# Second feed-forward pass of a conv-attention block: the last inner tile as f16 parts made by GpSimd

## What is computed

```python
def _bitlinear(x, W, b):
    y = einsum('btc,oc->bto', x, sign(W - groupmean(W))) + b
    # in 5 groups of 6 images: gamma = max|y| of the group
    return clip(y * 128 / (gamma + 1e-5), -128 + 1e-5, 128 - 1e-5)

def _L1_ffn_ref(x, W1, b1, W2, b2):       # 96 -> 384 -> 96
    h = _bitlinear(x, W1, b1)
    h = gelu(h, approximate=False)
    return _bitlinear(h, W2, b2)          # images 30 and 31 get zeros
```

## Time and profile before

| what | us |
|---|---|
| median of 3 runs (865.66 to 874.0) | 866.55 |
| the profiled execution | 865.46 |
| its span, first to last instruction | 863.7 |
| PE busy | 801.2 (93%) |
| DVE busy | 642.9 (74%) |
| ACT busy | 448.0 (52%) |
| POOL busy | 190.0 (22%) |

### The profile page before, as it was taken

The page is one execution under the profiler, slowest core; times in us unless marked ns, Lnnn a source line. Parts: engine busy times, 40 slices in busy tenths (PEclk is TensorE's granted clock), DMA queues, the critical chain, the costliest instruction groups (busy, mean ns, idle before and its releaser), DMA issues.

```text
span 863.7 us, 17964 instructions
## 1 busy us (share of the span) xinstructions
PE 801.2 (93%) x6053; PEld 621.3 (72%) x6053; DVE 642.9 (74%) x1998; ACT 448.0 (52%) x619; POOL 190.0 (22%) x218
## 2 busy tenths in 40 slices
PE   1889799999999999999999999999999799999991
PEld 1456478888888888888888888888888655555550
DVE  3875377877777777777777777777677457988997
ACT  0232335445445445445445445445444299988981
POOL 2750022322222322322322322322322000000000
PEclk9999889999999999999999999999999899999996
DMA  9930001100001100000100000110010010473433
GB/s 216 230 88 1 15 15 36 52 29 28 28 28 29 54 28 28 28 28 28 56 28 28 28 28 28 54 30 28 28 42 14 15 43 0 145 192 102 149 112 112
DMA packets 19886, 48.54 MB, mean 56 GB/s; under 512 B 4558, under 2 KB 4754, under 8 KB 19858
## 3 DMA queue, kind: packets, MB, share of 16 engines
q1 hardware_dynamic: 17024, 46.97, 19.6%
q10 hardware_dynamic: 2834, 1.21, 0.8%
HBM read 29.51 MB, written 18.67 MB: 56 GB/s over the span
## 4 chain that ended last, share of the span: by engine, by line
PE 75%; DVE 9%; issue 6%; ACT 3%; POOL 3%; ACTq 2%; DVEq 1%; POOLq 0%
PE slot L960 17%; PE slot L941 12%; PE slot L820 10%; PE slot L1006 9%; PE slot L1127 5%; PE slot L1098 4%; PE slot L967 4%; PE slot L970 4%; PE slot L955 3%; DVE stage L1492 2%; ACTq L600 1%; DVE y2max L1499 1%; DVE xn L1518 1%; ACT hT L773 1%; PE slot L1159 1%
## 5 line engine op out<-in xcount | busy, mean ns | idle before, releaser
L960 PE MATMUL slot<-w2s,hT 128*112 128x96 f32 x1344 | 162.7, 269 | 0.0
L1375 DVE TENSOR_SCALAR xh<-t,ln_mv,ln_rs 112x96 f32<-112x96 f32 x434 | 109.2, 322 | 60.0 <-POOL ln_rs L577 60.0
L960 PEld LDWEIGHTS slot<-w2s,hT 128*112 128x112 f32 x1344 | 141.6, 177 | 10.8
L710 ACT ACTIVATE hT<-slot,b1c,w_unit 128x784 f32<-128x784 f32 x96 | 95.8, 1004 | 95.6 <-PE slot L941 95.6
L717 ACT ACTIVATE stage<-slot,minus_one 112x768 f32<-112x768 f32 x64 | 52.5, 820 | 118.0 <-PE slot L1006 118.0
L550 POOL TENSOR_TENSOR xn_lo<-xn,xn_hi 96x784 f16<-96x784 f32 x32 | 53.4, 1669 | 247.5 <-ACT xn_hi L699 247.3
L577 POOL TENSOR_TENSOR ln_rs<-ln_ve,pow_half 112x7 f32<-112x7 f32 x62 | 91.9, 1482 | 4.8
L967 PE MATMUL slot<-big,W1b 99*128 (+1 forms) x360 | 89.4, 329 | 0.6 <-ACT hT L773 0.6
L970 PE MATMUL slot<-big,W1b 96*128 (+1 forms) x360 | 89.2, 328 | 0.0
L1381 DVE TENSOR_REDUCE ymax<-slot 128x784 f32 (+1 forms) x90 | 83.8, 960 | 6.2 <-PE slot L970 5.9
L1006 PE MATMUL slot<-qkvw,xh1T 97*112 97x192 f32 x448 | 85.7, 333 | 0.9 <-ACT xh1T L729 0.9
(11 more groups left out here) (189 smaller groups left out, 1358.6 us busy)
## 6 DMA issues: line engine op xcount, KB each, us to landing
out<-t2T SPq DMA_DIRECT2D x56, 294.0 KB, 3.2
xs<-in_x SPq DMA_DIRECT2D x32, 294.0 KB, 3.1
big<-in_x SPq DMA_DIRECT2D x7, 1176.0 KB, 12.4
xs<-out SPq DMA_DIRECT2D x24, 294.0 KB, 3.3
big<-out SPq DMA_DIRECT2D x1, 1764.0 KB, 11.3
out<-big SPq DMA_DIRECT2D x6, 294.0 KB, 2.6
big<-in_x SPq DMA_DIRECT2D x2, 588.0 KB, 5.6
con<-shape_consts ACTq DMA_DIRECT2D x1, 445.5 KB, 6.1
```

The costliest lines, as they stand in the source:

```text
L710: nc.scalar.activation(hT[:, t, :].rearrange("p (a n) -> p a n", a=2), halves((0, one, 2)[t], P), ACT.Relu, scale=w1_unit[:, t:t + 1], bia ...
L960: ins = mm(o[:, j, :], hT[:, t, j * TOK:(j + 1) * TOK], w2s[:, v, t, :], start=False, stop=t == TILES - 1, skip_group_check=True)
L1375: ins = V.tensor_scalar(dst[:, j, :], src[:, j, :], ln_mv[n][:, j, 0:1], ln_rs[n][:, j:j + 1], ALU.subtract, ALU.mult)
```

## The change

Tiles 1 and 2 now get their f16 parts from ACT (cast) and DVE (difference). Tile 0 gets them from GpSimd: DVE writes the clipped fp32 values of tile 0 to `h_clip`; GpSimd multiplies them by 1.0 into f16 (`h_hi` of tile 0) and then subtracts that from `h_clip` into f16 (`h_lo` of tile 0). PE takes the tiles in the order 1, 0, 2, all with the bf16 signs. `h_clip` is one buffer without a second copy: DVE waits before it writes it until GpSimd is through with the image before (`first_ready`). It takes the place of the raw expert weights, which are dead by then. GpSimd waits for `y2_ready` of two images back before it overwrites `h_hi`. `W2last` and `h_last` are gone.

```diff
--- before.py
+++ after.py
@@ -153,8 +153,10 @@
 
         con = sb("con", [P, K_END])
         ident = con[:, K_ID:K_ID + P]
-        w1_raw = sb("w1_raw", [P, TILES, C])
-        w2_raw = sb("w2_raw", [C, E, C])
+        first = sb("first", [P, HW])
+        w1_raw = first[:, 0:TILES * C].rearrange("p (t c) -> p t c", c=C)
+        w2_raw = first[0:C, TILES * C:TILES * C + HID].rearrange("p (e c) -> p e c", c=C)
+        h_clip = first
         w1_max = sb("w1_max", [P, TILES])
         w1_unit = sb("w1_unit", [P, TILES])
         w1_inv = sb("w1_inv", [P, TILES])
@@ -182,7 +184,6 @@
         fb1r = sb("fb1r", [C + PARTS, HID])
         W2_raw = sb("W2_raw", [C, HID])
         W2b = sb("W2b", [P, TILES, C], BF16)
-        W2last = sb("W2last", [P, C])
         fb2c = sb("fb2c", [C, 1])
         wsum = sb("wsum", [P, 2, QGROUPS])
         wmean = sb("wmean", [P, 2, QGROUPS])
@@ -261,13 +262,10 @@
         gel = hT
 
         stage16 = stage[:, :].bitcast(F16)
-        SPLIT = TILES - 1
-        part = SPLIT * HW
-        per_r = 2 * part + 2 * HW
+        part = TILES * HW
+        per_r = 2 * part
         h_hi, h_lo = ([stage16[:, r * per_r + n * part:r * per_r + (n + 1) * part].rearrange(
-            "p (t n) -> p t n", t=SPLIT) for r in range(2)] for n in range(2))
-
-        h_last = [stage16[:, r * per_r + 2 * part:(r + 1) * per_r].bitcast(F32) for r in range(2)]
+            "p (t n) -> p t n", t=TILES) for r in range(2)] for n in range(2))
         t2_tail = y2_all
         tc_buf = xs
         qv = xn
@@ -398,6 +396,9 @@
         tc_loaded = [sem(f"tc_loaded{r}") for r in range(2)]
         qv_ready = sem("qv_ready")
         hi_parts = sem("hi_parts")
+        hi_first = sem("hi_first")
+        first_ready = sem("first_ready")
+        pool_passed = sem("pool_passed")
         o_ready = sem("o_ready")
         tail_loaded = sem("tail_loaded")
         tail_clip = sem("tail_clip")
@@ -592,6 +593,22 @@
                     step(m, r)
             step(LAST // 2 - 1, 0)
             step(LAST // 2 - 1, 1, next_=False)
+
+            def first_parts(m, r):
+                b = 2 * m + r
+                pool.wait_ge(parts_ready, 3 * b + 1)
+                if not isinstance(b, int) or b >= 2:
+                    wait_apart(pool, y2_ready, b - 1, pool_passed)
+                nc.gpsimd.tensor_scalar(h_hi[r][:, 0, :], h_clip[:, :], 1.0, None, ALU.mult).then_inc(hi_first, 1)
+                pool.wait_ge(hi_first, b + 1)
+                nc.gpsimd.tensor_tensor(h_lo[r][:, 0, :], h_clip[:, :], h_hi[r][:, 0, :],
+                                        ALU.subtract).then_inc(first_ready, 1)
+
+            for r in range(2):
+                first_parts(0, r)
+            with pool.Fori(1, QIMAGES // 2) as m:
+                for r in range(2):
+                    first_parts(m, r)
 
 
         @block.scalar
@@ -742,7 +759,6 @@
                 if between:
                     gate_exps(0, 0)
                     act.wait_ge(signs_ready, 1)
-                    nc.scalar.copy(W2last[:, :], W2b[:, TILES - 1, :])
                     gate_exps(0, 1)
                     gate_exps(1, 0)
                 if attend:
@@ -775,7 +791,7 @@
 
             def gelu_hi(b, t, r):
                 wait_apart(act, gelu_ready, 3 * b + t + 1, act_passed)
-                if t == 0:
+                if t == 1:
                     wait_count(act, y2_ready, b - 1)
                     if not isinstance(b, int):
                         act.sem_inc(act_passed, 1)
@@ -792,9 +808,9 @@
                     if not (started and r == 0):
                         gelu_tile(g, b, 0)
                     gelu_tile(g, b, 1)
-                    gelu_hi(b, 0, r)
+                    gelu_hi(b, 1, r)
                     gelu_tile(g, b, 2)
-                    gelu_hi(b, 1, r)
+                    gelu_hi(b, 2, r)
                     if not (isinstance(b, int) and b == 0):
                         y2_out(b - 1)
 
@@ -1152,16 +1168,15 @@
                 if isinstance(b, int) and b == 0:
                     pe.wait_ge(t2T_evac, BATCH)
                 wait_count(pe, y2_evac, b)
-                for t in range(SPLIT):
-                    pe.wait_ge(parts_ready, 3 * b + t + 1)
+                for n, t in enumerate((1, 0, 2)):
+                    if t == 0:
+                        pe.wait_ge(first_ready, b + 1)
+                    else:
+                        pe.wait_ge(parts_ready, 3 * b + t + 1)
                     for part, src in enumerate((h_hi[r], h_lo[r])):
                         for h in range(2):
-                            mm(S[3][0:C, h, 0:HALF], W2b[:, t, :], src[:, t, h * HALF:(h + 1) * HALF],
-                               start=t == 0 and part == 0, stop=False, skip_group_check=True)
-                pe.wait_ge(parts_ready, 3 * b + TILES)
-                for h in range(2):
-                    ins = mm(S[3][0:C, h, 0:HALF], W2last[:, :], h_last[r][:, h * HALF:(h + 1) * HALF],
-                             start=False, stop=True, skip_group_check=True)
+                            ins = mm(S[3][0:C, h, 0:HALF], W2b[:, t, :], src[:, t, h * HALF:(h + 1) * HALF],
+                                     start=n == 0 and part == 0, stop=n == 2 and part == 1, skip_group_check=True)
                 ins.then_inc(y2_ready, 1)
 
             def group_scale_1(g):
@@ -1487,12 +1502,14 @@
 
             def split(m, r):
                 b = 2 * m + r
-                for t in range(SPLIT):
-                    dve.wait_ge(hi_parts, SPLIT * b + t + 1)
+                dve.wait_ge(gelu_ready, 3 * b + 1)
+                if not (isinstance(m, int) and m + r == 0):
+                    dve.wait_ge(first_ready, b)
+                V.tensor_scalar(h_clip[:, :], gel[:, 0, :], Q_CLIP, None, ALU.min).then_inc(parts_ready, 1)
+                for t in range(1, TILES):
+                    dve.wait_ge(hi_parts, 2 * b + t)
                     V.scalar_tensor_tensor(h_lo[r][:, t, :], gel[:, t, :], Q_CLIP, h_hi[r][:, t, :],
                                            ALU.min, ALU.subtract).then_inc(parts_ready, 1)
-                dve.wait_ge(gelu_ready, 3 * b + 3)
-                V.tensor_scalar(h_last[r][:, :], gel[:, 2, :], Q_CLIP, None, ALU.min).then_inc(parts_ready, 1)
 
             def y2_absmax(b):
                 dve.wait_ge(y2_evac, b + 1)
```

## The result

Four runs of the changed kernel have a median of 914.18 us (913.3 to 914.62); the kernel before stands at 869.58 beside them. The ratio is 1.0529 (95% interval 1.0493 to 1.0565): slower, by some 45 us of the medians. The forecast was 932 in a range of 883 to 946. The profiled execution took 914.49 us with a span of 912.6, against 865.46 and 863.7, so its own difference is 49 us. `y2_out` of the last image of the pass, 847.61 before, now starts at 896.46, which is 48.85 later. Of that, 2.8 us lie ahead of the pass: its first `gelu` starts at 693.19, where it was 690.40. The pass itself got 46.1 us longer, and that is the loss to be explained.

What follows compares the result with a forecast made beforehand. Bound before: PE and ACT in group 0, DVE in groups 1 to 4. Port turns of 29 x 6.19 plus 24 x 1.51, plus 2 for hand-offs, put the end 67.4 us later: 865.5 + 67.4, forecast 932 us, range 883 to 946.

Steps and rivals of the forecast that it cites:

- The port, exclusive in both directions: Second feed-forward pass: DVE's waiting forms and GpSimd's instructions exclude each other for whole instructions; only the 0.88 us maximum overlaps.
- The other by symmetry: SBUF port: rows showed DVE waiting for GpSimd; GpSimd waiting for DVE was assumed without a row.
- GpSimd's lengths: GpSimd's two added instructions: TENSOR_SCALAR 2.27 us and difference 1.67 us, 3.94 us an image.
- GpSimd's two follow one another: Second pass: waiting DVE forms and both GpSimd instructions add up, 6.19 us an image in group 0, 7.70 in groups 1 to 4.
- lower bound: Range's lower end, 883 us: GpSimd doesn't wait for a running DVE instruction, so two DVE turns an image lie beside it.
- Group 0 at 6.19: Image of group 0 in the second pass: 1.77 + 0.48 + 3.94 = 6.19 us, against 4.68 before.
- Mean of the L1492 differences well above 0.97 (near 2): Sign in the profile after: DVE's differences would average near 2 us in place of 0.97.
- near 5 tenths: Sign in the profile after: PE's busy share from slice 33 on, with ACT near 6.
- PE's 0.65 us an image brings nothing: PE's products in the second pass: 19.5 us freed in all, none reaching the end; rival of full gain, 846 us, chance 0.04.
- The clock: Rival, chance 0.06: PE at half clock in the second pass needs 8.06 us an image, 10 us more, 942.
- The cheap first instruction: Rival, chance 0.28: GpSimd's first instruction takes 0.84 us like a CAST, port sum falls 41.5 us, 891.
- No exclusion: Rival, chance 0.12: GpSimd's 3.94 us run beside DVE in the second pass; time stays 865 us, within 1%.

Runs made afterwards that it cites:

- shadow run: Kernel before, with the two GpSimd instructions of each image added on spare buffers and nobody waiting for them: 908.88 us, ratio 1.0465.
- early clip: Changed kernel with the next image's clip issued on DVE right behind the maximum, ahead of `qv` and the output: 912.21 us, ratio 1.0491.
- warm run: Changed kernel with 24 unread products of 104 columns ahead of PE's wait for GpSimd in every even image: 913.67 us, ratio 1.0540.
- two buffers: Changed kernel with a second clip buffer, so a clip waits for GpSimd's parts of two images back: 936.43 us, ratio 1.0766.

## Why the prediction was right, and where its size was off

- *The port, exclusive in both directions.* Right, and now shown in rows of this pass: DVE's TENSOR_SCALAR and its forms with two SBUF inputs wait for GpSimd, GpSimd waits for them, the maximum waits for neither. "The other by symmetry" was a guess, and 4.20 for 1.67 us bears it out. Not right was that the lock is "held for a whole instruction": the TENSOR_TENSOR bears it out, the TENSOR_SCALAR doesn't (0.69 of 2.17 us for a two-input form), and the measurement decides. The shadow run shows that the port by itself can cost 41 us.
- *GpSimd's lengths.* Right: 2.27 was forecast for the TENSOR_SCALAR and its shortest takes 2.17; 1.67 for the difference is 1.67. The slope between two widths of the same operation was a good instrument. So was the choice of operation: the CAST row's 0.84 is the length of a CAST and of no TENSOR_SCALAR here.
- *"GpSimd's two follow one another" with the DVE forms.* This is the mis-sized term. The forecast let the TENSOR_SCALAR hold the port for its whole 2.27 us. In the images read it costs DVE 0.64. DVE's port-bound forms take 1.77 + 0.48 + 0.62 + 0.89 = 3.76 us of an image, and 3.76 + 0.64 + 1.67 = 6.07 in place of 7.70; 6.66 and 6.65 us were the images of the shadow and of the early clip, in which the maximum lies beside no difference of GpSimd and some 0.6 us come on top. The changed kernel has 6.59, in another way: there the maximum can lie beside the difference (836.07 and 836.57), and DVE idles instead. My evidence was one MEMSET and one TENSOR_TENSOR, both of which hold to the end; I carried it to a form that was not among them.
- *Why the number still came out near: two errors of opposite sign.* With 0.64 in place of 2.27 my own sum gives 932 - 29 x 1.63 = 885 us, 29 below the measured 914. The other error is that I let DVE never idle, and put all hand-offs at 2 us. From the first `gelu` of the pass to its last `y2_out` (690.40 to 847.61 before, 693.19 to 896.46 after) DVE idles 53.4 us, where it idled 23.0. Of these 30 us more, 18.9 stand ahead of the clip, waiting for GpSimd, and 11.7 ahead of the maximum, behind PE and ACT. That they filled the gap is luck. The lower bound has a slip too: two turns of 0.89 are 1.78 and not 1.7 us, which makes it 880.
- *Group 0 at 6.19.* It took 5.34. What binds there is the loop clip, 2.69, 1.67, clip with its hand-offs; of the port only 0.52 us is in it, the TENSOR_SCALAR's wait for a difference. I had named the wait and what stands behind it, and then priced it only through the port.
- *"Mean of the L1492 differences well above 0.97 (near 2)".* Wrong as a sign: 1.12. GpSimd did more of the waiting (23 us, DVE 12.4), and idle time ahead of clip and maximum holds the rest. The maximum at 0.96 and the undisturbed main pass were right, PE "near 5 tenths" was too low: it stands at 7 for the most part, partly because its products last longer at half clock.
- *PE's 0.65 us an image brings nothing.* Nothing of it arrived in any run, but no run shows it by itself: with GpSimd the port and the loop bind, and without it ACT's extra cast does.
- *The clock.* The half level comes, mechanism as told, but its cost is hidden where the warm run lifted it: from 790 to 850 us it gains nothing. *The cheap first instruction* was judged by its length, and its length was the wrong quantity. The instruction is long and its hold is short. With a CAST in its place, the rival's own case, the kernel takes 900 us (that rival's sum is 891), 14 less than with the TENSOR_SCALAR though both hold a difference off for the same 0.69: the length counts too, through the loop. *No exclusion* is out.

What stays open: why GpSimd sometimes gets its turn between two DVE forms that run back to back (2.49 us for a pair at 832.99) and sometimes not (1.85 at 826.39, and the 4.20 above). The order of turns decides how port and loop share the loss in a given image. How they share it over the whole pass can be read from DVE, which sets the pace before (the pass from its first `gelu` to its last `y2_out`; idle time is the pass less DVE's busy time in it, held-up time the means of its groups less those of the kernel before, times their counts):

| kernel | pass, us | DVE idle | DVE held up |
|---|---|---|---|
| before | 157.2 | 23.0 | 0 |
| changed | 203.3 | 53.4 | 12.4 |
| clip early | 202.8 | 27.3 | 40.5 |
| CAST | 189.4 | 24.7 | 29.6 |
| both on spare buffers | 199.1 | 14.3 | 51.9 |

The changed kernel loses mainly by idling, 30 us of the 46; held up at the port it is for 12.4, and the rest is records that no longer overlap. The early clip turned nearly all of those waits into holds. The CAST took 28.7 us of idling away and added 17.2 of holds; among the edits that leave GpSimd its work, it alone gave time back that is clear of the noise. The idle time can't be put down to the loop alone, since GpSimd's waits for the port (23 us) lengthen the loop.

## What to carry to other kernels

An engine that idles is not free if it shares a port with the engine that bounds the stage: add its hold of the port to that engine's period first, and ask afterwards whether its own work fits, and who waits for it. The hold is a quantity of its own, not the instruction's length, and a shadow (the same instructions on spare buffers, with nobody waiting for them) prices it in one run, before any data is moved over. Its sum need not be the sum of the real kernel: here 41 stood against 45, but with the holds on DVE at 52 us in one and 12 in the other. And where two limits feed each other, removing a wait on one side can come back as a hold on the other (clip early: 912 for 914, two buffers: 936); shortening the work of the helper helped (CAST: 900).

## What the runs showed of the hardware that was not expected

- A one-step TENSOR_SCALAR of GpSimd, f32 to f16 at 784 elements, takes 2.17 us. It keeps a DVE form with two SBUF inputs off the port only until 0.69 us after its start (0.97 us at 714.59 is unheld); a form with one input waits once more near its end (clip 1.00 us for 0.56 at 723.47). A CAST of 0.84 us holds for the same 0.69, and a TENSOR_TENSOR of 1.67 us almost to its end (1.48 us of delay for a clip issued just behind its start).
- DVE forms that follow one another without a gap can keep a waiting GpSimd instruction out: 4.20 us for 1.67 of work. The kernel in which DVE lost its wait ahead of the clip was 22 us slower.
- GpSimd's elementwise forms differ by more than three: at 784 elements, the CAST 0.84 us, the TENSOR_SCALAR with one step 2.17, with two steps 2.89 (on 96 partitions).
- An instruction's recorded time contains its wait for the port, so a long mean can be the other engine's work; the shortest of a group is its own length.
